# The FP4 stage's third product behind all gate and up segments of its step

## What is computed

```
def fp4_linear(x, w):
    return jnp.einsum('bsk,nk->bsn', fp4_quant_dequant(x), fp4_quant_dequant(w))

def _L1_ffn_ref(x, w_gate, w_up, w_down):      # I = 704, H = 256
    gate = fp4_linear(x, w_gate)
    y = fp4_linear(x, w_up)
    h = jax.nn.silu(gate) * y
    return fp4_linear(h, w_down)

x = x + _L1_ffn_ref(_layernorm(x, axis=-1), w_gate, w_up, w_down)
```

## Time and profile before

| | value |
|---|---|
| time, median of 3 runs | 977.89 us (972.24 to 978.2) |
| the profiled execution's own time | 974.39 us |
| its span, first to last instruction | 972.6 us |
| mean granted TensorE clock over the span | 0.977 of full speed |
| PE busy over the span | 914.9 us (94%) |
| DVE / ACT / POOL busy | 775.4 (80%) / 482.0 (50%) / 461.1 (47%) us |
| segments, L1522 (576 matmuls) | 140.0 us |
| down product, L1542 (384 in the trace) | 89.4 us |

### The profile page before, as it was taken

How to read it: one execution, slowest core, us unless ns; L and a number is a source line. 1 busy time by engine, 2 the same in 40 slices (tenths; PEclk the granted TensorE clock), 3 DMA queues, 4 the chain that set the end, 5 groups by cost and what they waited for, 6 DMA issues and landing times. The chain is left out here.

```text
span 972.6 us, 20302 instructions
## 1 busy us (share of the span) xinstructions
PE 914.9 (94%) x7332; PEld 815.6 (84%) x7332; DVE 775.4 (80%) x2108; ACT 482.0 (50%) x1019; POOL 461.1 (47%) x663
## 2 busy tenths in 40 slices
PE   6899999999589999998799999999979999999997
PEld 4889999998479999997689888988867888888885
DVE  4799999997477677754778889889868988989874
ACT  2453433433198888886343334333454454444442
POOL 1223343341266666654212333333247777777762
PEclk9799999999699999999989999999999999999999
DMA  9020000000000000000000000000000000000000
GB/s 343 37 99 2 2 2 1 2 3 1 1 1 1 1 1 1 1 1 26 29 2 2 2 2 2 1 2 2 1 1 1 23 23 23 1 23 23 23 22 23
DMA packets 6083, 18.32 MB, mean 19 GB/s; under 512 B 864, under 2 KB 2784, under 8 KB 5472
## 3 DMA queue, kind: packets, MB, share of 16 engines
q1 hardware_dynamic: 5264, 16.52, 4.4%
q10 hardware_dynamic: 720, 0.50, 0.2%
HBM read 12.83 MB, written 4.19 MB: 17 GB/s over the span
## 5 line engine op out<-in xcount | busy, mean ns | idle before, releaser
L875 PE MATMUL a_psO<-vblk,a_prob 128*128 128x51 f32 (+1 forms) x1280 | 150.4, 273 | 0.0
L875 PEld LDWEIGHTS a_psO<-vblk,a_prob 128*128 128x128 f32 x1280 | 150.0, 194 | 0.0
L1522 PE MATMUL f_psGU<-wgu,f_xTs 128*128 128x512 f32 (+1 forms) x576 | 140.0, 388 | 3.1 <-ACT f_silu L1472 3.1
L515 DVE TENSOR_REDUCE a_mx<-a_psS 128x4 f32<-128x308 f32 x256 | 114.9, 469 | 25.8 <-PE a_psS L791 22.9
L711 ACT COPY a_xTs<-a_psQ 128x256 f32<-128x256 f32 x64 | 23.8, 372 | 209.8 <-PE a_psQ L800 209.8
L722 ACT ACTIVATE a_prob<-a_psT 128x512 f32<-128x512 f32 (+1 forms) x192 | 101.0, 526 | 40.4 <-PE a_psT L847 39.7
L1522 PEld LDWEIGHTS f_psGU<-wgu,f_xTs 128*128 128x128 f32 x576 | 102.9, 190 | 18.0 <-DVE f_xTs L1267 3.4
L847 PE MATMUL a_psT<-ident,a_shifted 128*128 128x128 f32 x640 | 106.9, 282 | 10.9 <-ACT a_prob L722 7.9
L523 DVE TENSOR_TENSOR a_shifted<-a_psS,a_mx 128x308 f32<-128x308 f32 x256 | 114.2, 466 | 0.0
L1104 PEld LDWEIGHTS s_psY<-w,s_hid 128*128 128x128 f32 x768 | 100.6, 189 | 9.1 <-POOL s_hid L1020 3.6
L672 POOL TENSOR_TENSOR a_rstd<-a_mv,expo 128x1 f32<-128x1 f32 x64 | 15.2, 238 | 194.5 <-DVE a_mv L599 194.5
(11 more groups left out here) (158 smaller groups left out, 1813.9 us busy)
## 6 DMA issues: line engine op xcount, KB each, us to landing
out_x<-x SPq DMA_DIRECT2D x8, 512.0 KB, 2.6
x<-in_x SPq DMA_DIRECT2D x3, 1024.0 KB, 13.3
w<-in_w SPq DMA_DIRECT2D x1, 2304.0 KB, 8.9
w<-in_w SPq DMA_DIRECT2D x2, 1024.0 KB, 18.0
a_mask<-in_mask SPq DMA_DIRECT2D x4, 308.0 KB, 3.9
wat<-in_att SPq DMA_DIRECT2D x1, 1024.0 KB, 21.1
x<-in_x SPq DMA_DIRECT2D x1, 768.0 KB, 9.3
wat<-in_att SPq DMA_DIRECT2D x2, 256.0 KB, 5.6
```

What stands on the lines that cost most here:

```text
L515: nc.vector.tensor_reduce(mx[:, u, j * BH:(j + 1) * BH], psS[j][:, 0:BH * KV].rearrange("p (h k) -> p h k", k=KV), AX.X, ALU.max).then_inc ...
L875: mm = nc.tensor.matmul(psO[:, CH[c] * VW:(CH[c] + n) * VW], prob[:, v, c * P:(c + 1) * P], vblk[:, t // R, c * NJ * VW:(c * NJ + n) * VW] ...
L1522: mm = nc.tensor.matmul(psGU[:, n0:n1], xTs[:, u, a, k * P:(k + 1) * P], wgu[:, b, k, n0:n1], start=(n == 0), stop=(n == len(TERMS) - 1))
```

## The change

The block of step 2 above, with its waits, is cut out from its place between segment 0 and the x transposes, and put behind segments 1 and 2, ahead of the transposes into psA.

```diff
@@ -1532,16 +1532,6 @@
                 wait(pe, xT_low, i + 1)
                 wait(pe, silu_ready, i)
                 products(u, 0)
-            if valid(i - 3):
-                t = i - 3
-                wait(pe, x_done, t)
-                wait(pe, hT_copied, 2 * t + 1)
-                for c in range(NF1):
-                    if c == HTA:
-                        wait(pe, hT_copied, 2 * t + 2)
-                    mm = nc.tensor.matmul(psY[:, 0:D], hTs[:, 1 - u, c * P:(c + 1) * P], wdT[:, c, :],
-                                          start=(c == 0), stop=(c == NF1 - 1))
-                mm.then_inc(y_mm, 1)
             if valid(i + 1):
                 wait(pe, xres_ready, i + 2)
                 wait(pe, xT_low, i + 1)
@@ -1554,6 +1544,16 @@
                 wait(pe, hid_ready, i)
                 products(u, 1).then_inc(gu_mm, 1)
                 products(u, 2).then_inc(gu_mm, 1)
+            if valid(i - 3):
+                t = i - 3
...
+                mm.then_inc(y_mm, 1)
             if valid(i - 2):
                 t = i - 2
                 if t == 0:
```

More of the change, by code:

```diff
@@ L1556, in step @@
                 products(u, 2).then_inc(gu_mm, 1)
+            if valid(i - 3):
+                t = i - 3
+                wait(pe, x_done, t)
+                wait(pe, hT_copied, 2 * t + 1)
+                for c in range(NF1):
+                    if c == HTA:
+                        wait(pe, hT_copied, 2 * t + 2)
+                    mm = nc.tensor.matmul(psY[:, 0:D], hTs[:, 1 - u, c * P:(c + 1) * P], wdT[:, c, :],
+                                          start=(c == 0), stop=(c == NF1 - 1))
+                mm.then_inc(y_mm, 1)
             if valid(i - 2):
```

## The result

The changed kernel takes 993.45 us (median of 4 runs, 988.73 to 997.56) against 975.07 us of the kernel before, measured beside it (median of 4, 970.05 to 978.2). The ratio is 1.0192, with a 95% interval of 1.0119 to 1.0264: slower, by 18.4 us. The sum of the prediction gave 993.1 us. The profiled execution took 995.58 us, with a span of 993.8, against 972.6 before.

What follows compares the result with a forecast made beforehand. TensorE set the pace, with VectorE close behind. Twenty steps of 8.27 us (165.4) and eight of 7.98 (63.8) moved the end by +18.7 us from 974.39 to 993.1 us; range 985 to 1002.

Steps and rivals of the forecast that it cites:

- The sum: Steps 2 to 21 at 8.27 us, 22 to 29 at 7.98; end moves +18.7 us from 974.39 to 993.1.
- The ring: One-step loop: down product, residual, bn_stats, x_low, transposes into psB, segments, next down product; 8.27 us a step.
- handover from VectorE to TensorE: From the end of x_low to TensorE's transposes into psB: taken as 0.07 us, bounds 0.00 and 0.15.
- The late steps: From step 22 on, without bn_stats: 7.98 us a step, eight steps making 63.8 us.
- the loop over the down-scaled x: Two-step loop: product, residual, hidden, down-scaled x, x transposes; 16.40 us or 8.20 a step, 7.98 from step 22.
- The waits: Expected profile: TensorE waits for x_low some 28 times, about 0.9 us each; residual for the product, about 1.2 each.
- the rival of the clock: TensorE's clock falls in every step from its idle gaps: up to 1.03 us each, 1022 us; chance 0.03.
- the loops close behind: Two-step loops through hidden, over h_down at 8.12 us a step and over the down-scaled x at 8.20.
- the wait for h_down: TensorE waiting for GpSimd's h_down before psA: costs about 0.23 us a step before the change, nearly gone after.
- the loops hit one another: Rival: shifts and GpSimd's deviations make loops collide; with 0.3 us more a step, 1001 us; chance 0.07.
- The faster rival: VectorE's answer is ready behind psA, so a step is TensorE's own 7.31 us: 968 us; chance 0.03.
- a cover of 1.35 us: TensorE work needed between down product and psB transposes to hide VectorE's answer; the change leaves 0.44 us.

Runs made afterwards that it cites:

- A cover of 1.49: Changed order, but with the down product between segments 1 and 2, against the kernel before the change: 974.13 us, ratio 1.0016.

## Why the prediction was right

**The ring.** All its legs were found, and nearly all had the right size. Product to residual: 2.79 forecast, 810.12 - 807.33 = 2.79 measured. Residual to the end of x_low: 1.08 and 811.21 - 810.12 = 1.09. psB to segment 0: 0.19 and 0.16. Segment 0 to the next product: 4.14 and 815.66 - 811.51 = 4.15. Only the handover from VectorE to TensorE, for which a row of GpSimd stood in, was too small: 0.07 forecast, 811.35 - 811.21 = 0.14 measured, close to its upper bound. With the three other hundredths added (1.09, 0.16, 4.15) that is the difference between 8.27 and 8.33.

**The late steps.** 7.98 was forecast, and 7.98 is the measured mean, but that is luck. The forecast took it from the loop over the down-scaled x. In the trace these steps wait for x_low, so it is the one-step ring that holds them: 7.93 plus 0.07 for the longer handover gives 8.00, and seven steps took 8.00 to 8.01. The mean comes down to 7.98 only by the last of the eight, at 7.78. The loop over the down-scaled x was sized too long: 0.95 from residual to hidden, where the trace has 918.96 - 918.13 = 0.83.

**The sum.** The last hidden moved from 953.25 to 974.26:

```profile
973.93 0.42 DVE L1240 TENSOR_TENSOR x<-x,f_psY 128x256 f32<-128x256 f32 x1 [2.30 <-PE f_psY L1554]
974.26 0.88 DVE L1288 TENSOR_TENSOR f_hid<-f_silu,f_psGU 128x704 f32<-128x704 f32 x1
```

That is 21.0 us, against 18.7 forecast. Of the 2.3 more, 1.3 are the twenty steps of 8.33 instead of 8.27, and about 1.2 were there already at the first down product, 740.66 against the 739.49 of the sum; nearly all of that arose ahead of the stage, in a part of the program that is alike in both. The profiled spans, 993.8 and 972.6, lie 21.2 apart. Measured by medians of runs side by side, the change costs 18.4 us. So the mechanism and the step were right. That the forecast of 993.1 came within 0.4 us of the median of 993.45 is luck: the runs of one kernel alone spread over 8.8 us, and the interval of the ratio leaves 12 to 26 us for the change.

**The waits.** Right: TensorE stands in front of psB 27 or 28 times, VectorE's residual in front of the product in all steps, for some 1.5 us where 1.2 were forecast. The clock stays at 1.00. The step is 8.33 - 7.31 = 1.02 us longer than TensorE's own work, but the trace shows only 0.54 us of it as idle in front of psB and 0.07 in front of psA in the step above; the rest is matmul tails that no longer overlap with the next group. So the rival of the clock falls for idle spells of this size, and the Trainium skill's warning in "TensorE: Matmul & The Clock Gate" on small idle spells between groups of matmuls did not come true here. Right too: the loops close behind. Wrong: that the wait for h_down would be nearly gone. It is 16.9 us in 27 weight loads, more than the 10.8 in 15 before, since hidden now starts late, behind the residual. But it costs nothing of its own: the 0.2 us or so that psA waits in a common step lie inside the time for which psB would wait anyway. From residual to hidden it was 1.2 us without shifts, not the 1.40 taken between the floor and a row with shifts, and 1.42 with them, not 1.55. That leaves the second loops more room than thought, and the rival "the loops hit one another" did not come about.

**The faster rival.** It named a cover of 1.35 us as its point of decision. A cover of 1.49 did remove the wait for x_low, but not the loss, since hidden sits in the same queue. The point was right for the ring and incomplete for the kernel. No run lies between 0.44 and 1.49, so the 1.35 itself was not tested.

## What to carry to other kernels

When a producer is moved later in one engine's list, look at its consumer's list on the other engine: not the consumer itself matters (here the residual, which nobody was waiting for), but what is queued behind it and for which the first engine waits. Add up the ring of one step from start-to-start distances, and compare it with the busiest engine's own work in a step; then add up the next longer rings, since a mended ring only falls to the next one. And a consumer moved later needs the same look backwards: who waits to reuse the buffer that it reads? Where the same instruction is added inside the supposed ring and at the same place in the kernel without it, as here, the two costs (all of it, and nothing) tell the ring from a mere lateness.

## What the runs showed of the hardware

A VectorE instruction that reads two tiles in SBUF can be held by GpSimd. L1299 works on 44 columns and takes 0.20 us, 193 to 205 ns for all 32 in the changed kernel, but up to 515 ns in the kernel before and 660 in the run with the product between the segments. There it ends 0.06 us behind GpSimd's instruction that runs beside it:

```profile
817.88 0.65 DVE L1299 SCALAR_TENSOR_TENSOR f_ham<-f_ham,f_tiny 128x44 f32<-128x44 f32 x1
```

```profile
817.85 0.62 POOL L1371 TENSOR_TENSOR f_xval<-f_xhat,f_xinv 128x256 f32<-128x256 f32 x1
```

This one started 0.03 us behind GpSimd's. Where the two started within 0.01 us of one another, in the same run, VectorE's took its usual time and GpSimd's 0.69 instead of 0.62 us:

```profile
825.62 0.19 DVE L1299 SCALAR_TENSOR_TENSOR f_ham<-f_ham,f_tiny 128x44 f32<-128x44 f32 x1
```

```profile
825.61 0.69 POOL L1371 TENSOR_TENSOR f_xval<-f_xhat,f_xinv 128x256 f32<-128x256 f32 x1
```

In the traces of all eleven kernels together, from 720 us on, L1299 took over 0.22 us 113 times. Each time it ended 0.05 to 0.07 us behind a GpSimd instruction that had started before it, L1371 or L1386 in 110 cases and L1380 in three. Where it started 0.04 us or more ahead of one of L1371 or L1386, that one didn't lengthen it. So the later of the two seems to be held until the other is through, not slowed down.

The Trainium skill ("GPSIMD Engine Reference", section "1. Specifications") says that GpSimd shares its interfaces to SBUF with VectorE and contends with VectorE instructions that have two SBUF inputs; these rows agree, with 0.45 us as the price of one meeting, on the two-step loop of that run. No run here moved this meeting by itself, so it is read from the traces alone, as a coincidence in time.
